# Shared experts fed from the attention stage: turned halves stored, weights split there, and slots named in two parts

## The reference

```python
xn = layernorm(x)
x  = x + attention(xn, 16 heads of 16, causal) + moe(xn)
xn = layernorm(x)
x  = x + scan_layer(xn) + moe_with_latent(xn)

def moe(xn):                          # 8 experts, hidden 352
    scores = softmax(xn @ gate_w.T)
    idx = top_k(scores + gate_b, 2)   # each token goes to two experts
    h_e = silu((xn @ w1_e + b1_e) * (xn @ w3_e + b3_e))
    y   = sum over the two chosen e of scores[e] * (h_e @ w2_e + b2_e)
    return y + shared(xn)             # shared: an expert for every token
```

## Time and profile before

| | |
|---|---|
| median of 3 runs | 1236.97 us (1232.79 to 1238.09) |
| profiled execution | 1237.58 us, its span 1235.8 us |
| PE busy | 1124.0 us (91%) |
| DVE busy | 914.1 us (74%) |
| ACT busy | 682.2 us (55%) |
| POOL busy | 529.9 us (43%) |
| granted PE clock, mean | 0.977 of 2.4 GHz |

### The profile page before, as it was taken

One profiled execution on the slowest core, in us unless ns is written; L12 is line 12 of the kernel. 1 busy time (PEld: TensorE's weight loads), 2 busy tenths in 40 slices (PEclk: granted clock), 3 DMA queues, 4 the chain that ended last, 5 costly groups with the idle time before them and its releaser, 6 DMA issues. The chain is left out here.

```text
span 1235.8 us, 26934 instructions
## 1 busy us (share of the span) xinstructions
PE 1124.0 (91%) x8964; PEld 751.5 (61%) x8965; DVE 914.1 (74%) x2224; ACT 682.2 (55%) x1478; POOL 529.9 (43%) x751
## 2 busy tenths in 40 slices
PE   4789999999999966998999999997999999999998
PEld 2345555555555435887999888883555555546555
DVE  4778898888887826885756667674877977977866
ACT  2256565665556544665656666655554654664553
POOL 5343333424333228833444443332635546447314
PEclk9689999999999997999999999998999999999999
DMA  4437524445234106656232453442231241332302
GB/s 137 82 72 215 108 45 95 95 78 102 45 79 87 18 35 190 192 161 197 76 126 81 123 163 122 121 141 69 81 126 41 97 129 42 102 94 72 107 8 97
DMA packets 98276, 125.17 MB, mean 101 GB/s; under 512 B 14480, under 2 KB 87888, under 8 KB 97168
## 3 DMA queue, kind: packets, MB, share of 16 engines
q1 hardware_dynamic: 87184, 105.07, 31.9%
q0 software_dynamic: 6912, 18.88, 5.5%
q10 hardware_dynamic: 4096, 0.14, 0.2%
HBM read 84.70 MB, written 39.19 MB: 100 GB/s over the span
## 5 line engine op out<-in xcount | busy, mean ns | idle before, releaser
L479 ACT ACTIVATE p<-bank 128x384 f32<-128x384 f32 (+1 forms) x384 | 191.5, 530 | 186.0 <-PE bank L855 119.6
L688 DVE TENSOR_REDUCE neg_max<-bank 128x1 f16<-128x384 f32 (+3 forms) x352 | 219.6, 640 | 65.0 <-PE bank L843 62.2
L397 POOL TENSOR_SCALAR_AFFINE_SELECT p<-p 128x256 f32<-128x256 f32 x256 | 103.6, 409 | 245.4 <-ACT p L479 244.7
L121 PE MATMUL xbank<-gT_hi,w_hi 128*128 128x256 f16 (+1 forms) x636 | 175.0, 275 | 15.3 <-DVE w_lo L1448 6.0
L122 PE MATMUL xbank<-gT_lo,w_hi 128*128 128x256 f16 (+1 forms) x636 | 174.7, 275 | 0.0
L123 PE MATMUL xbank<-gT_hi,w_lo 128*128 128x256 f16 (+1 forms) x636 | 174.6, 274 | 0.0
L840 PE MATMUL bank<-k_stack,q_stack 96*128 96x384 f16 (+3 forms) x512 | 133.5, 313 | 20.1 <-DVE neg_max L688 12.6
L1382 ACT ACTIVATE a<-xbank,b 128x256 f32<-128x256 f32 x159 | 74.3, 468 | 65.9 <-PE xbank L123 62.4
L1293 POOL DMA_INDIRECT fetched<-xn_dram,token_now x80 | 81.4, 1017 | 42.9 <-POOL token_now L1289 30.7
L1934 POOL TENSOR_TENSOR up_lo<-up_sq,up_hi 128x512 f16<-128x512 f32 x32 | 43.2, 1378 | 126.6 <-ACT up_hi L1991 126.6
L1467 DVE SCALAR_TENSOR_TENSOR prod<-xbank,b,a 128x256 f32<-128x256 f32 x159 | 73.8, 476 | 31.4 <-ACT a L1382 23.7
(11 more groups left out here) (304 smaller groups left out, 3065.5 us busy)
## 6 DMA issues: line engine op xcount, KB each, us to landing
w_bc<-wT_dram SPq DMA_DIRECT2D x8, 2048.0 KB, 8.3
y_routed_dram<-y SPq DMA_DIRECT2D x37, 256.0 KB, 2.1
w<-in_w SPq DMA_DIRECT2D x11, 704.0 KB, 6.8
pack<-in_pack SPq DMA_DIRECT2D x12, 342.0 KB, 4.0
xr<-in_x SPq DMA_DIRECT2D x8, 512.0 KB, 7.3
xn_dram<-xn SPq DMA_DIRECT2D x8, 512.0 KB, 3.1
qk_hi_dram<-qk_hi SPq DMA_DIRECT2D x16, 256.0 KB, 2.8
qk_lo_dram<-qk_lo SPq DMA_DIRECT2D x16, 256.0 KB, 2.6
```

Of the source, the lines that this page charges most:

```text
L121: pe.matmul(out, hi_a(c), hi_b(c), start=first and x == 0, stop=False)
L397: pool.affine_select(out=diagonal, in_=diagonal, pattern=[[0, 2], [1, P]], compare_op=ALU.is_ge, fill=0.0, base=0, channel_multiplier=-1). ...
L479: act.activation(p32[:, s // GH % 2, s % GH, cols], s_bank[n][:, 0:cols.stop - cols.start], ACT.Exp).then_inc(p_exp.sem, 1)
L688: dve.tensor_reduce(neg_max[:, g % 2, 0:GH * TT].rearrange("p (h t) -> p h t", t=TT)[:, heads[0]:heads[-1] + 1, j], a_bank[c % 2][:, 0:len ...
```

## The change

A class `Carried` holds what attention hands to the experts: the split shared weights, the shared bias, and two buffers `turned` for the transposed halves of a tile. They take the place of the attention's float32 weights and of `q32`, which use the same memory while they are needed.

In attention, SP stores the transposed halves of each batch (`store_xT`, two transfers of 256 KB), after `load_x` and before the q and k of that batch. At the start of the last batch SP loads the shared weights into buffers that are free by then, and turned tiles 0 and 1. ACT and DVE split the weights in the last batch, at steps 31, 33, 36, 38 and 33, 35, 38, 40. SP's list no longer waits for the last x1 store to land; the experts wait for it where they read it.

In the experts, the shared tiles read `turned`, which SP loads two tiles ahead (`load_turned`), and have no transposes and no `x_part`. The prologues load and split no shared weights. `find_slots` is cut in two: seven steps stay in the prologue, the rest is `name_slots` and follows DVE's `gated` of tile 0. All 64 `in_column` are DVE's, eight a tile. Expert 1's weights are loaded at tile 1 and not 0, expert 2's at tile 3 and not 1. The counts of several signals shift by one, since expert 0 is no longer split here.

```diff
-PLACED_BY_DVE = 56
-PLACED_A_TILE = 7
+PLACED_BY_DVE = 64
+PLACED_A_TILE = 8
+AT_SHARED = (3, 5, 8, 10)
...
+            def store_xT(b):
+                sp.wait_ge(xT_lo_s.sem, xT_lo_s.at(b))
+                for k, of in enumerate((xT_hi, xT_lo)):
+                    sp.dma_start(dram["xnT"][b][:, k], of[:, :, :]).then_inc(xT_stored.sem, 16)
+
+            def load_shared():
+
+                sp.wait_ge(xb_ready.sem, xb_ready.at(NB - 1))
+                sp.wait_ge(xn_ready.sem, xn_ready.at(NB - 1))
+                sp.dma_start(w13_32[0], w["w13"][0][0:P, :]).then_inc(shared_in_loaded.sem, 16)
+                sp.wait_ge(xT_psum.sem, xT_psum.at(NB - 1))
+                sp.wait_ge(xn_stored.sem, xn_stored.at(NB - 1))
+                sp.dma_start(w13_32[1], w["w13"][0][P:2 * P, :]).then_inc(shared_in_loaded.sem, 16)
+                sp.wait_ge(qk_stored.sem, qk_stored.at(2 * NB - 1))
...
+                for n in range(2):
+                    sp.dma_start(carried.turned[:, n], turned_tile(dram["xnT"], n)).then_inc(turned_loaded[n].sem, 16)
...
-            sp.wait_ge(x1_stored.sem, x1_stored.at(NB - 1))
+            sp.wait_ge(x1_stored.sem, x1_stored.at(NB - 2))
+            sp.wait_ge(xT_stored.sem, xT_stored.at(NB - 1))
...
             def x_high(b, c, of):
...
+                act.wait_ge(xT_stored.sem, xT_stored.at(b - 1))
...
+            def split_shared(n):
+                loads = shared_in_loaded if n < 2 else shared_out_loaded
+                act.wait_ge(loads.sem, loads.at(0))
+                if n < 2:
+                    act.activation(carried.w13_hi[:, n, :], w13_32[n], ACT.Copy).then_inc(w_hi.sem, 1)
...
+                    elif at - 28 in AT_SHARED:
+                        split_shared(AT_SHARED.index(at - 28))
...
+            def load_turned(n, tile, read):
+
+                sp.wait_ge(gu_psum.sem, gu_psum.at(read))
+                sp.dma_start(turned[:, n % 2], turned_tile(dram["xnT"], tile)).then_inc(turned_loaded[n % 2].sem, 16)
...
                 gated(i, bias, 2)
+                if is_int(i, 0):
+                    name_slots()
...
             def tile(i, u, before, stage, to_split=None):
-                pe.wait_ge(gT_lo_s.sem, gT_lo_s.at(i))
...
+                n = shared_place(i, stage)
+                if n is None:
+                    pe.wait_ge(gT_lo_s.sem, gT_lo_s.at(i - HEAD_TILES))
+                else:
+                    pe.wait_ge(turned_loaded[n % 2].sem, turned_loaded[n % 2].at(n // 2))
+                gate_up(i, u, 0, n)
+                gate_up(i, u, 1, n)
+                if next_routed(i, stage):
+                    x_transposes(i + 1)
+                gate_up(i, u, 2, n)
...
-                pe.wait_ge(column_placed.sem, column_placed.at(0))
```

239 lines of the change are left out of this document (129 added, 110 removed).

## The result

The changed kernel took 1229.95 us, median of seven runs (1228.36 to 1231.04), against 1236.97 for the kernel before on the same chip (seven runs, 1232.79 to 1243.53). The ratio is 0.9946, 95% interval 0.9924 to 0.9969. The forecast was 1219, with a range of 1214 to 1229: the direction was right, but 7.0 us were gained where 18 were forecast, and the time lies just outside the range. The profiled execution took 1228.36 us (span 1226.6), against 1237.58 (1235.8) before: 9.2 us less, where 17.8 were forecast.

What follows compares the result with a forecast made beforehand. The head was taken as bound by PE, the seam by waits. Gains of 19.8 us less 2.0 paid by attention gave 17.8: span 1235.8 to 1218.0, forecast 1219 us, range 1214 to 1229.

Steps and rivals of the forecast that it cites:

- (1): Seam: SP no longer waits for the last x1 store to land; stage starts at 461.1 instead of 463.56.
- (2): Seam: PE needs only turned tile 0 and split weights; first product at 461.1 against 473.24, idle gap 1.7 us.
- one of my signs of being wrong: Seam: the forecast counts as wrong if PE's clock falls there.
- Rival C: Same steps but dearer: POOL at 0.76 or attention paying 6, 1223; both plus late biases, 1228.7; clock fall 1221; chance 0.25.
- Steps (3) to (5): Head start: tile 0's biases land at 465.3, DVE's gated products end at 467.0, name_slots takes 2.95 us, POOL starts at 470.2.
- The middle of attention: Later batches: storing turned rows costs 0.2 us in all, bounds 0 and 4.
- (7): Head: PE's own way to the table, shared tiles at 5.90 us with DVE nearly level, ends at 515.3.
- (6): Head: POOL's 64 in_lane at 0.70 us plus two more end at 517.3, setting the table, 17.7 us earlier.
- one of my own conditions for being wrong: Head: the forecast counts as wrong if the table isn't waiting for POOL.
- Attention: Attention stage: turned-row stores and weight splits together cost 2.0 us.
- The tail: Tail shared tiles: dropped transposes gain 4 x 0.43 = 1.7 us, bounds 0 and 1.7 if row gathers take it back.
- D: Seam opens early but tile 0 waits for late biases; table 12 us earlier, attention paying 6: 1230 to 1237; chance 0.05.

Runs made afterwards that it cites:

- the four edits, first run: Changed kernel plus expert 1's weights in tile 0, splits behind the last exps, first batch's turned-row stores late, tail's turned loads early: 1249.07 us, 0.9867 to the kernel before.

## Why the prediction was right and wrong, step by step

The profiled execution came out 8.6 us over the forecast for it. 2.1 of that is there when the stage starts (465.24 where 463.1 was forecast), 5.6 more when the table starts (61.84 us after the stage's start instead of 56.2), 1.7 more from the table to layer 1, and layer 1 gave 0.8 back.

**Right.** Steps (1) and (2): the stage starts without the store, and the first product 0.33 us after it, at the upper clock. The clock was in part luck: PE's idle gap was 2.13 us, and in seven of the twelve profiles with that gap the clock fell at the seam, one of my signs of being wrong. Rival C had priced such a fall at 2 us; it cost 2.2. Steps (3) to (5): biases in 3.5 us (4.2 forecast), name_slots 2.92 us (2.95), POOL's start 8.5 us after the stage's (9.1). The middle of attention costs nothing. What I gave no price of its own, and should have, is the clock behind step (1): the old wait is worth 2.4 us by itself, and in the profile with it the head is 3.3 us longer as well.

**The step that failed: (7).** "Tile 2 can start at 474.0 and end 479.9; six more tiles at 5.90 give 515.3" takes every turned tile for there when PE wants it, and DVE for slightly faster than PE. Neither held. The load of expert 1's weights moved from tile 0 to tile 1; I priced the loads that were taken away from the seam and not where this one came to stand: behind a store that waits for tile 0's output, and ahead of the turned load that PE needs next. PE stood 5.31 us, and thirteen products at half clock took 1.4 us more. With the weights in tile 0 the head is 61.57 us instead of 65.46, so 3.9 us are SP's order; the other 2.8 of these 6.7 did not come back. I put that down to DVE's pace, which then binds instead; no run shows it by itself. DVE's tile is 6.50 us beside POOL (6.02 alone), not "nearly level with 5.90": five tiles at 6.50 and one at 6.02 are 3.1 us over six at 5.90. In the forecast's terms, counted from the stage's start, step (7) ends at 54.2 us; measured are 61.84, and 57.95 with the weights in tile 0. So this term was short by 7.6: 3.9 for SP's order, 3.7 for the pace and small waits. The forecast's table was only 5.6 early because step (6) had put POOL at 56.2.

Part of the error could be read off the kernel before. I had priced the placements by a row at 530.65, where POOL had ended (1.62 us for seven). Beside POOL seven took 1.94 us (timeline of DVE in the kernel before):

```profile
490.21 1.94 DVE L1534 TENSOR_SCALAR in_column<-lanes_half,pos_f,ids 128x114 f16<-128x114 f16 x7
```

**Step (6).** POOL took 0.666 us an instruction (42.61 for 64), not 0.70, and did not set the table; that was one of my own conditions for being wrong. The Trainium skill, "SBUF — State Buffer", section "SBUF: two separate sides", describes the port pair of the two engines as an exclusive lock that can stop either. I had taken POOL for the one that loses. The traces put part of the loss on DVE: with the weights in tile 0 a placement took 0.336 us in the median from 480 to 500, beside POOL, and 0.305 once POOL had ended. So both lose: POOL's lanes took 0.67 us where eight beside a nearly idle DVE had taken 0.58 each, and eight placements 2.32 us instead of 1.84. With seven placements a tile instead of eight DVE's tile was 0.35 us shorter.

**Attention** paid 3.97 us instead of 2.0. The start cost 1.5, not 0.3 and beyond my bound of 1: the q/k stores, behind 512 KB of turned rows, brought the first stack load from 25.33 to 26.91, and DVE's first maxima from 32.28 to 33.35, so DVE hid 0.5 us of it and not 1 or more. The splits cost 1.1 (1.5 forecast), the middle 0 (0.2); and 1.4 is a fall of the clock among the exps, for which no term stood.

**The tail.** From the table to layer 1 0.45 of 2.1 us were gained, and the tail alone got 2.9 us longer. "If the row gathers that follow don't take it back" named the bound but not the mechanism. One wait that the trace shows is again a turned load behind a store in SP's list (1.93 us); how much of the 2.9 us goes with it, one profile on one chip says (28.07 us without it). On two chips something else stands there that no view names.

**Rivals.** The result, 1229.95, lies between C, whose sum at its worst was 1228.7, and D's 1230 to 1237. C had attention dearer and the clock, but not the place; D had the table 12 us earlier, which is nearer to the 7.9 measured than the forecast's 17.7, by late biases that did not come. D's own sum was too small: a table 12 us earlier, 2.1 us behind it and 6 lost in attention make 8.1 us, not 6 to 7. What was missing among them is a rival of SP's order, with its place: tile 4.

**What stays open.** What brings the clock down is not settled beyond this: it falls behind idle waits of PE, at least once in the last 30 us of attention or in tile 0 in every kernel without added products but one (the four edits, first run), and not from 452 to 482 where the waits were filled. Why the same kernel falls at the seam in one profile and not in the next is open, and so is what the engines stand still for in the tail on two chips.

## What to carry to other kernels

When a change moves a large load to another place in a queue that is worked off in order, list what now stands directly behind it, who waits for that and when, and compare the issue with the time of need: this price was 4 us of the head, twice what the forecast gave to all of attention. When a wait is taken out ahead of a dense stretch of TensorE, count the clock that it may cost as well as the wait, and look at more than one profile before you count on it. And when work is moved between two engines that slow each other, measure the pace of both beside each other; the row of the one alone is a lower bound.

## What the runs showed of the hardware

- A wait of 4.55 us on PE ahead of tile 0 was followed by 0.51 of full clock for 6 us; the same wait filled with products that nobody reads left it at 1.00. With 2.13 us of idleness at the same seam the clock fell in seven profiles of twelve, with 0.6 us in none of five.
- Eight placements on DVE in the changed kernel: 1.84 us once POOL had ended, up to 2.33 beside it. POOL's 128x114 column took 0.87 us beside a dense DVE, its 128x128 lane 0.65 to 0.69 in the mean of the 64. Two patterns were seen, 2.32 us for DVE's eight with 0.65 for the lane, and 2.11 with 0.69.
- The 256 KB loads of turned tiles took 3.0 us to land at the least, 4.3 in the median, 8.6 behind 1 MB of weights; SP's issue of the last of these weight loads took 1.92 us, where the two ahead of it took 0.43 and 0.47.
- Two of the four chips took 413 to 421 us for layer 1 in nine kernels, where the others took 388 to 391, and only they show waits over 0.6 us without a releaser in the tail (up to 2.70 us on PE).
